# Attention's sums and results turned in 32x32 blocks by VectorE, in place of 128x128 transposes on TensorE

## The reference

```python
def attention(x, Wqkv, bqkv, Wo, bo):
    q, k, v = jnp.split(x @ Wqkv + bqkv, 3, axis=-1)      # 16 heads of 16
    scores = jnp.einsum('bhid,bhjd->bhij', q, k) * 0.25
    scores = scores + alibi_causal_bias(512, 16)          # -(i-j)*slope, -inf for j > i
    out = jnp.einsum('bhij,bhjd->bhid', softmax(scores), v)
    return out.reshape(b, s, 256) @ Wo + bo

def ffn(x, W_up, W_gate, W_down):                         # each W made ternary first
    hidden = silu(x @ W_up.T) * (x @ W_gate.T)
    return hidden @ W_down.T

x = layernorm(x + attention(x))
x = layernorm(x + ffn(x))
```

## Time and profile before

| | us |
|---|---|
| median of 3 runs | 624.6 |
| the runs | 620.04, 624.6, 696.24 |
| span of the profiled execution | 619.3 |
| busy in it: PE / PEld / DVE / ACT / POOL | 583.6 / 342.5 / 494.4 / 318.8 / 299.0 |

### The profile page before, as it was taken

The page is one execution under the profiler, slowest core; times in us unless marked ns, Lnnn a source line. Parts: engine busy times, 40 slices in busy tenths (PEclk is TensorE's granted clock), DMA queues, the critical chain, the costliest instruction groups (busy, mean ns, idle before and its releaser), DMA issues.

```text
span 619.3 us, 12888 instructions
## 1 busy us (share of the span) xinstructions
PE 583.6 (94%) x4012; PEld 342.5 (55%) x4012; DVE 494.4 (80%) x1258; ACT 318.8 (51%) x593; POOL 299.0 (48%) x504
## 2 busy tenths in 40 slices
PE   5789888999999999999999999999999999999995
PEld 3344354664656555674556646575556646446674
DVE  5388968996799868989599877989599877993766
ACT  2129713459247644477246653476345753576262
POOL 1306695346275535465174543654264452654234
PEclk9789998999999999999999999999999999999998
DMA  6965715005462073502653064601644054600101
GB/s 158 289 175 206 211 51 161 23 29 163 122 172 66 3 229 115 166 1 83 161 166 100 1 199 123 160 28 52 186 144 127 1 166 105 206 2 3 35 1 35
DMA packets 47724, 68.49 MB, mean 111 GB/s; under 512 B 4857, under 2 KB 43641, under 8 KB 44793
## 3 DMA queue, kind: packets, MB, share of 16 engines
q1 hardware_dynamic: 47691, 68.08, 37.5%
HBM read 38.44 MB, written 29.36 MB: 109 GB/s over the span
## 4 chain that ended last, share of the span: by engine, by line
PE 78%; DVE 5%; ACT 5%; POOL 5%; issue 4%; DMA 2%; SPq 0%; POOLq 0%; DVEq 0%
PE ring L698 17%; PE max_bank L613 10%; PE acc L647 9%; PE ring L635 9%; PE ring L590 8%; PE acc L715 7%; PE ring L597 4%; ACT probs L772 4%; PE ring L671 4%; PE max_bank L618 2%; PE ring L655 2%; POOL probs L1042 2%; PE ring L684 1%; POOL tern_down L1085 1%; PE max_bank L715 1%
## 5 line engine op out<-in xcount | busy, mean ns | idle before, releaser
L772 ACT ACTIVATE probs<-ring 128x512 f32<-128x512 f32 x320 | 170.7, 606 | 45.6 <-PE ring L635 44.0
L1042 POOL TENSOR_SCALAR_AFFINE_SELECT probs<-probs 128x256 f32<-128x256 f32 (+1 forms) x320 | 120.5, 401 | 130.1 <-ACT probs L772 129.4
L896 DVE CUSTOM_DVE_ANT_0 max_bank<-max_bank,causal_wide 128x384 f32<-128x384 f32 (+1 forms) x256 | 157.2, 637 | 15.3 <-PE max_bank L613 12.2
L613 PE MATMUL max_bank<-k_stack,q_stack 112*128 112x384 bf16 (+3 forms) x512 | 123.4, 304 | 5.9 <-DVE neg_max L896 2.8
L1078 POOL TENSOR_TENSOR hidden_lo<-hidden,hidden_hi 128x512 f16<-128x512 f32 (+1 forms) x72 | 75.1, 1050 | 63.6 <-ACT hidden_hi L803 63.3
L635 PE MATMUL ring<-q_stack,k_stack 114*128 114x512 bf16 (+3 forms) x512 | 103.7, 300 | 1.6 <-DVE attn L921 0.5
L791 ACT ACTIVATE gating<-ring,tanh_scale 128x512 f32<-128x512 f32 (+1 forms) x72 | 45.8, 639 | 74.0 <-PE ring L698 74.0
L647 PE MATMUL acc<-probs,v_ones 128*32 128x512 f32 (+3 forms) x1024 | 79.9, 437 | 2.8 <-POOL probs L1042 2.8
L613 PEld LDWEIGHTS max_bank<-k_stack,q_stack 112*128 112x128 bf16 x512 | 46.5, 98 | 54.0 <-DVE neg_max L896 15.3
L900 DVE TENSOR_REDUCE neg_max<-max_bank 128x2 f32<-128x512 f32 (+1 forms) x96 | 63.7, 686 | 10.4 <-PE max_bank L618 8.7
L635 PEld LDWEIGHTS ring<-q_stack,k_stack 114*128 114x128 bf16 x512 | 44.5, 97 | 49.4 <-issue 17.0
(11 more groups left out here) (107 smaller groups left out, 866.0 us busy)
## 6 DMA issues: line engine op xcount, KB each, us to landing
q_stack<-qk_scratch SPq DMA_DIRECT2D x15, 768.0 KB, 6.1
k_stack<-k_slots SPq DMA_DIRECT2D x15, 768.0 KB, 7.8
qk_scratch<-qk_parts SPq DMA_DIRECT2D x16, 384.0 KB, 3.0
k_slots<-qk_parts SPq DMA_DIRECT2D x16, 384.0 KB, 2.6
xin<-x_dram SPq DMA_DIRECT2D x8, 512.0 KB, 3.5
qk_scratch<-qk_parts SPq DMA_DIRECT2D x16, 256.0 KB, 3.2
k_slots<-qk_parts SPq DMA_DIRECT2D x16, 256.0 KB, 2.3
res<-x_dram SPq DMA_DIRECT2D x8, 512.0 KB, 3.4
```

The lines of the kernel that those rows point to most:

```text
L613: mm = pe.matmul(max_bank[k][:, width * i:width * (i + 1)], q_stack[0:MAX_ROW, 4 * g + h, P * tile:P * (tile + 1)], k_stack[0:MAX_ROW, 4 * ...
L772: rg.drained(act.activation(probs[:, g % 2, n, :], rg.bank(step)[:, :], ACT.Exp), step)
L896: dve.tensor_tensor_reduce(scores, scores, causal_wide[:, SEQ - width:SEQ], -1.0, LOWEST_START, ALU.add, ALU.min, neg_max[:, g, first_col: ...
L1042: return pool.affine_select(out=v, in_=v, compare_op=ALU.is_ge, fill=0.0, base=0, pattern=([[0, blocks]] if blocks > 1 else []) + [[1, P]] ...
```

## The change

- `nt` and `at` leave TensorE, and with them the copies of ScalarE and VectorE between. VectorE turns an `acc` bank in 32x32 blocks (`turn.g`, into `pv_t`): in each block the 16 results and the sum of one head stand for 32 tokens. `nt_out.g` normalises there, into `mixed`, two quads side by side in a block, and `at.f`, now on VectorE, turns `mixed` back, into `attn_t`.
- The features in `attn_t` then stand in another order, so `wo` is loaded with its rows to fit, by 8 DMAs during the first batch (`load_wo.1`). The fold of the value bias into the output bias needs the plain order, and reads it from `attn_t`, which is free then (`load_wo.0`).
- `v` makes two token tiles in one ring bank, in 2 steps where there were 4, and `v_out` copies both at once. In the loop's table `v.0` stands where `v.1` stood, behind `x1t`, and `v.1` where `v.3` stood; the places of the old `v.0` and `v.2` are empty.
- The ring is filled 8 times fewer for a batch. All other steps keep their order.

```diff
-RING_STEPS = ("tx", "qk", "v", "at", "x1t", "up", "gate", "mt", "nt", "exp", "bias_fold", "wsum")
+RING_STEPS = ("tx", "qk", "v", "x1t", "up", "gate", "mt", "exp", "bias_fold", "wsum")
 LOOP_ORDER:
-    mt_out.3 qk.0 exp.2.8 nt.0 ln2 exp.2.9 qk_out.0 pv.1.2 part_write.0.0 pv.1.3 nt_out.0 exp.3.0 exp.3.1 store
-    split.0 exp.3.2 qk.1 exp.3.3 part_write.0.1 exp.3.4 nt.1 exp.3.5 qk_out.1 exp.3.6 exp.3.7 exp.3.8 nt_out.1
-    exp.3.9 pv.2.0 split.1 pv.2.1 pv.2.2 pv.2.3 pv.3.0 nt.2 part_write.1.0 part_write.0.2 pv.3.1 pv.3.2
-    part_write.1.1 nt_out.2 pv.3.3 at.0 nt.3 nt_out.3 part_write.1.2 wo.0.0 at.1 wo.1.0 wo.0.1 wo.1.1 stack_read.0
+    take.3.9 pv.1.0 take.3.10 pv.1.1 ffn_stats.1 exp.2.6 mt.3 exp.2.7 mt_out.3 qk.0 exp.2.8 turn.0 ln2 exp.2.9
+    qk_out.0 pv.1.2 part_write.0.0 pv.1.3 nt_out.0 exp.3.0 exp.3.1 store split.0 exp.3.2 qk.1 exp.3.3 part_write.0.1
+    exp.3.4 turn.1 exp.3.5 qk_out.1 exp.3.6 exp.3.7 exp.3.8 nt_out.1 at.0 exp.3.9 pv.2.0 split.1 pv.2.1 pv.2.2
+    pv.2.3 pv.3.0 turn.2 part_write.1.0 part_write.0.2 pv.3.1 pv.3.2 part_write.1.1 nt_out.2 pv.3.3 turn.3 nt_out.3
+    part_write.1.2 wo.0.0 at.1 wo.1.0 wo.0.1 wo.1.1 stack_read.0
 SP:
                     elif kind == "load_wo":
-                        sp.dma_start(wo[:, :, :], w_o.rearrange("(t p) n -> p t n", p=P)).then_inc(weights_in[1], 16)
+                        if step[1] == 0:
+                            sp.dma_start(attn_t[:, :, 0:HID], w_o.rearrange("(t p) n -> p t n", p=P)).then_inc(weights_in[1], 16)
+                        else:
+                            rows = w_o.rearrange("(f e h d) n -> f h e d n", f=FT, e=2, d=DH)
+                            for f in range(FT):
+                                for h in range(4):
+                                    sp.dma_start(wo[32 * h:32 * (h + 1), f, :], rows[f, h]).then_inc(wo_in, 16)
 PE:
                     elif kind == "v":
-                        t = step[1]
                         for f in range(FT):
-                            mm = pe.matmul(bank[:, 0:HID], x_t[:, f, P * t:P * (t + 1)], wqkv[:, f, 2 * HID:3 * HID],
-                                           start=(f == 0), stop=(f == FT - 1))
+                            for i in range(2):
+                                mm = pe.matmul(bank[:, HID * i:HID * (i + 1)], x_t[:, f, P * (2 * u + i):P * (2 * u + i + 1)],
+                                               wqkv[:, f, 2 * HID:3 * HID], start=(f == 0 and i == 0), stop=(f == FT - 1),
+                                               skip_group_check=True)
-                    elif kind == "nt":
-                        for t in range(TT):
-                            mm = pe.transpose(bank[:, P * t:P * (t + 1)], pv_t[:, g % 2, P * t:P * (t + 1)], ident[:, :])
-                    elif kind == "at":
-                        for t in range(TT):
-                            mm = pe.transpose(bank[:, P * t:P * (t + 1)], attn[:, t, P * f:P * (f + 1)], ident[:, :])
                     elif kind == "wo":
                         if u == 0:
-                            rg.wait_drained(pe, ("at", f))
-                            pe.wait_ge(weights_in[1], 32)
+                            at_least(pe, attn_turned, FT, b, f + 1)
+                            pe.wait_ge(wo_in, 16 * 4 * FT)
 ACT:
-                    elif kind == "pv" and step[1] < 2 and step[2] == TT - 1:
-                        act.activation(pv_t[:, g % 2, :], acc[g % 2][:, :], ACT.Copy).then_inc(acc_drained[g % 2], 1)
-                    elif kind == "at":
-                        rg.drained(act.activation(attn_t[:, step[1], :], rg.bank(step)[:, :], ACT.Copy), step)
 DVE:
-                    elif kind == "pv" and step[1] >= 2 and step[2] == TT - 1:
+                    elif kind == "turn":
                         g = step[1]
+                        if not (first and g == 0):
+                            at_least(dve, mixed_done, QUADS, b, g - 1)
                         at_least(dve, acc_filled[g % 2], 3, b, g // 2 + 1 - acc_skipped(name))
-                        dve.tensor_copy(pv_t[:, g % 2, :], acc[g % 2][:, :]).then_inc(acc_drained[g % 2], 1)
+                        dve.transpose(pv_t[:, g % 2, :], acc[g % 2][:, :]).then_inc(acc_drained[g % 2], 1)
                     elif kind == "nt_out":
-                        heads = rg.bank(nt)[:, :].rearrange("p (s c) -> p s c", c=32)
+                        heads = pv_t[:, g % 2, :].rearrange("p (s c) -> p s c", c=32)
                         dve.reciprocal(inv_sum[:, g % 2, :, :], heads[:, :, DH:DH + 1]).then_inc(inverted, 1)
-                        rg.drained(dve.tensor_tensor(
-                            attn[:, :, 4 * DH * g:4 * DH * (g + 1)].rearrange("p t (h d) -> p t h d", d=DH),
-                            heads[:, :, 0:DH].rearrange("p (t h) d -> p t h d", t=TT),
...
+                        dve.tensor_tensor(
+                            mixed[:, g // 2, :].rearrange("p (s c) -> p s c", c=32)[:, :, DH * (g % 2):DH * (g % 2 + 1)],
+                            heads[:, :, 0:DH], inv_sum[:, g % 2, :, :].broadcast_to([P, TT * 4, DH]),
+                            ALU.mult).then_inc(mixed_done, 1)
+                    elif kind == "at":
+                        f = step[1]
+                        at_least(dve, mixed_done, QUADS, b, 2 * f + 2)
+                        dve.transpose(attn_t[:, f, :], mixed[:, f, :]).then_inc(attn_turned, 1)
```

176 lines of the change are left out of this document (84 added, 92 removed).

## The result

The changed kernel takes 640.7 us (median of 4 runs, 637.8 to 642.5), the kernel before 623.3 beside it (median of four runs; 621.9 of the three that agree). The ratio is **1.029, with a 95% interval of 1.024 to 1.034**: slower, and 23 us over the 617.4 predicted, outside the range of 607 to 631. The fourth run of the kernel before, at 696 us, stands far from the others and is left out of the ratio. The profiled execution took 640.5 us with a span of 638.8, 19.5 us more than before.

A forecast was written before the change was run, and what follows sets the result against it. TensorE's instructions were taken as the bound. Terms of -1.5 (batch 0), -2.0 (batch 1), +0.9 (loop) and -2.3 us (batch 7) sum to -4.9, taking 622.3 to 617.4 us; range 607 to 631 us.

The forecast's parts named there:

- batch 0, -1.5 us: End of batch 0: VectorE's last chain releases the last two products at 82.7 instead of 84.22, saving 1.5 us.
- The loop, +0.9 us: Five iterations: the stack read lands last, behind a later `split.1`, costing 0.2 us each, 0.9 us in all.
- 0.8 us later than before, 0.3 us of which reach `pv.3`: Loop iteration's end: `qk_out.1` starts 0.8 us later on VectorE behind added transposes, delaying `pv.3` by 0.3 us.
- Batch 7, -2.3 us: Last batch, with no next batch to feed: the end of its attention gets shorter, saving 2.3 us.
- Batch 1, -2.0 us: Batch 1: its end shrinks from 7.9 to 6.3 us and ScalarE loses two copies, saving 2.0 us.
- The value products: Value products made in pairs, the first now behind `x1t`: no effect on the time.
- The transpose: One VectorE transpose of 128x512 was taken to last 0.69 us, like the copy it replaces.
- rival B: VectorE's transposes are dear: at 1.2 us each the kernel takes 630.7 us; chance 0.17.
- TensorE's saving: 24 transposes a batch leave TensorE: at most 3.8 us a batch, 30 us in all.
- The loads of `wo`: Eight DMAs in batch 0, over 30 us ahead of the first projection: no cost, 1 us if that cover is gone.
- Rival A: The read isn't late and each loop iteration gains up to 1.8 us: 607.5 us; chance 0.15.
- Rival C: TensorE's granted clock falls after its new waits at batch ends, costing 10 us: 627.6 us; chance 0.10.

The follow-up runs named there:

- e1: The changed kernel with GpSimd's three operations of `ternary.2` left out of batch 0: 627.6 us, ratio 1.010 to the kernel before.
- e2: The changed kernel with VectorE's `ternary.1` moved behind `at.1` in batch 0: 637.7 us, ratio 1.026.
- e9: The changed kernel with GpSimd's `ternary.2` in twelve short operations, six of them moved to batch 1, and `ternary.1` behind `at.1`: 628.6 us, ratio 1.012.
- e3: The kernel before with `ternary.1` moved from ahead of `nt_out.2` to behind it in batch 0: 628.7 us, ratio 1.012.
- e4: The changed kernel with `turn.1`, `nt_out.1` and `at.0` moved behind `split.1` in the loop: 632.6 us, ratio 1.017.
- e5: The changed kernel with `nt_out.0`, `turn.1`, `nt_out.1`, `at.0` and `ln2` behind `split.1` in the loop, and `store` behind `stack_read.0`: 639.3 us, ratio 1.028.
- e14: The changed kernel with the changes of e9 and e4 together: 622.7 us, ratio 1.003.
- e7: The changed kernel with `ternary.1` behind `at.1`, and GpSimd's `ternary.2` made to wait until `ternary.1` is done: 637.4 us, ratio 1.024.
- e8: The changed kernel with the orders of e5, e6 and e7 together: 634.7 us, ratio 1.019.
- e11: The changed kernel with the changes of e9 and e10 together, and `v.0` ahead of `max.0.0` in batch 0: 630.3 us, ratio 1.014.
- e6: The changed kernel with the first pair of value products (`v.0`) moved ahead of `max.0.0`, its copy behind `take.0.0`: 638.4 us, ratio 1.028.
- e10: e4 with the loop's `qk_out.0` and `qk_out.1` done by ScalarE instead of VectorE: 641.3 us, ratio 1.032.

## Why the prediction was wrong

**The step that failed: batch 0, -1.5 us.** It said that VectorE's last chain "some 1.1 us behind for the added transposes, would release them at 82.7". It took the durations of before for operations that now stand elsewhere and read elsewhere. The last products were released at 99.3, and batch 0 took 15.4 us more. Of these about 11.4 are the three operations held beside GpSimd (e1), 2.4 the stretch ahead of `qk_out.0`. Three things were not looked at: that GpSimd's 7.47 us operation begins at 76.84, 1.6 us behind `ternary.1`; that `nt_out` reads SBUF instead of PSUM in the new kernel; and how far VectorE falls back, 2.2 us by `ternary.0` even in e1, for the 1.1 taken over the whole chain. So the term would have been +1.9 even without GpSimd, and not -1.5. What the second is worth by itself isn't tested: one of the last two products was held in the changed kernel and in e2, none in e9. The trace of before did show the price: the four normalising operations of batch 1 take 3.42 us from 94.94 on, beside GpSimd, and 1.38 in the loop. e1, e2, e3 and e9 show from four sides that the hold by GpSimd is the cause.

**The loop, +0.9 us: the mechanism right, the size wrong.** The read does land last, as predicted, and e4 shows that `turn.1` and `at.0` ahead of `qk_out.1` and `split.1` are the reason: with them behind, the loop is back at the time of before. The term measured +4.95 us over the five iterations. The wait for the read is smaller than the predicted 1 to 2 us, at 0.66 to 0.98. The mis-sized part is `qk_out.1`, "0.8 us later than before, 0.3 us of which reach `pv.3`": the scores of `exp.3.6` wait 1.44 us for it where there was no such wait at that place, and `pv.3` 0.93 us where it was 0.36. The first iteration alone has 2.1 of the 4.95 us, and e4 leaves it at that. It has a wait of 0.74 us for the DMA of the maxima that the others haven't; in e5 and e14 it hasn't, and takes 71.1 and 71.4 us instead of 72.5. The rest is open.

**Batch 7, -2.3 us: measured +1.2.** The end of its attention came as worked out: from the last value product to the last product of the projection 5.3 us (598.2 to 603.5) for 6.7, with a wait of 1.3 us for `at.1` in it. But TensorE comes there 1.2 us later than before, after waits of 1.0 us for the read and 0.7 and 0.8 us for maxima, so the attention gains 0.2 us and not 2.3; no run isolates these waits. The FFN behind takes 1.4 us more (35.2 for 33.9), and that is the clock, which fell to 0.50 behind TensorE's waits of 1.34 and 0.97 us and within one of 0.73 (at 600.7, 606.7 and 608.1):

```profile
606.00:612.00 6.00, 4.22 (x22) 2.86 (x23) 2.98 (x9) 1.54 (x3) 0.79 (x1) 0.72 0.00 0
```

The same place in the kernel before (588 to 594) has 1.00. Of the runs with the change, those where the clock fell there take 35.2 to 35.4 us for it (e7, e8, e9, e11, e14) and those where it held 34.1 (e1, e2, e4, e5, e6, e10).

**Batch 1, -2.0 us: measured -3.5, by luck.** e3, which turns no block, has -3.3: what batch 1 gains is that GpSimd is done with `ternary.2` by then. Beside that the changed kernel is 0.3 us shorter than e3 there.

**The value products, "Nothing".** In the loop nothing shows (e6). In batch 0 the stretch with them is 2.4 us longer than before, and longer at the same clock too (32.3 for 31.2 at 0.95); the term was put at nothing without a look at the order of batch 0. Two small slips in the sums change nothing: batch 7's parts add up to 2.5 and not 2.3, the loop's to 1.0 and not 0.9.

**What held.** The transpose: 0.709 and 0.711 us against 0.69 taken, so rival B falls. The estimate of 0.71 that the prediction worked out from the Trainium skill's "VectorE: DVE Perf Modes" and "Trainium Kernel Development and Optimization", at the one element a cycle in each lane of "Vector Engine (DVE) Microarchitecture Reference", section 3.8, agrees with the rows. TensorE's saving: 3.0 us a batch in the loop, of at most 3.8. The loads of `wo` are waited for nowhere. VectorE is busy for 526.9 us and not 515, since the 11.4 us of holds count as busy time of the held operations: no view of waits shows them, only a duration far from that of its like. Rival A, that the gain is kept, was refuted by the waits of the loop. Rival C: the clock did fall, behind the wait of 16.3 us and once more in batch 7, and it was lower in the first stretch of batch 0, but it stayed at 1.00 at the ends of the loop's iterations, behind waits of up to 1.44 us; "nearly all of TensorE's gain turns into a wait" was right for the loop, and was far from the largest term.

## What to carry to other kernels

Before an operation is moved, look at what GpSimd does at that time: a duration taken from one place of a trace holds only where the same neighbour is at work, and a long GpSimd operation can hold a short one of VectorE on the critical path; cut it in pieces (3 us gained even in the kernel before). Where a queue serves two deadlines, work moved off a third engine should be put in order by those deadlines first and counted second: the same operations in another order were worth 5 us in the loop (e4), and in a third order 2 us (e5). And a stage that is run once (batch 0) deserves its own timeline, since its order may rest on an edge that no steady iteration shows, and a change of order that costs the loop nothing can cost it something.

## What the runs showed of the hardware

**VectorE and GpSimd exclude each other for some operations.** Beside a running GpSimd operation, the comparison from float32 to float16 (1.3 us) took 5.6 to 5.9 us, the one with two inputs in SBUF (2.4 us) 5.7 to 6.0, a product of two SBUF tensors (0.42) 2.9 to 4.0, and `var_eps` (0.17) up to 2.0. Not held were transposes, from PSUM (0.70) and from SBUF (0.71, in e9 at 82.30, beside GpSimd's operations at 80.94 and 82.60), and sums and maxima with an input in PSUM (z 0.69 at 85.46 in the kernel before, its three maxima 2.02 together at 89.08). It works the other way too: GpSimd's first operation takes 7.47 us where VectorE's operation of 2.37 us started just ahead of it and 5.45 in e7, where nothing did. The Trainium skill says this in "SBUF — State Buffer", section "Who interferes with whom": the two share a pair of ports, and whoever comes second waits for the whole instruction, if VectorE's reads two SBUF inputs (and GpSimd's reads SBUF) or runs in a two-port mode; no run here shows the ports themselves. The long holds and the transposes without one are as that rule has them. The short products are so only in part: in e2 one was let go 1.5 us before the recorded end of GpSimd's operation, and the next (at 85.62) wasn't held, and in e9 neither was, at 80.47 and 81.84 (0.42 us each), beside GpSimd's operations of 77.36 to 80.96 and 80.94 to 82.51. There the measurement decides.

**The granted clock.** It fell to 0.50 behind waits of TensorE of 16.3 us and 4.8 us (e1, from 83.8 to 87.4), and to 0.60 on average behind one of 4.76 (e7). Waits of 1.4 to 1.5 us in an otherwise full iteration left it at 1.00, while in the kernel before one of 1.22 us in batch 1 was followed by 0.72, and in batch 7 of the changed kernel three of 1.34, 0.97 and 0.73 us went with 0.50, from about 608 to 611.5. The length of one wait doesn't settle it: in e10 and in e11 each of the five iterations has the same wait of 1.81 us, and the clock fell behind one of the five (to 0.50 for about 3 us), and held behind the other four.
